# Query feature maps turned before the output projection in segment attention

## The reference

```
for each segment of 128 tokens (8 a sequence), 16 heads of 64:
    sq  = elu(q) + 1                                  # query feature map
    mem = mem + sq^T v;   zc = zc + sum(elu(k) + 1)
    att_dot = softmax(q k^T / 8) v
    att = gate * (sq mem / (sum(sq) * zc)) + (1 - gate) * att_dot
    out = att @ Wo                                    # output projection
x = layernorm(x + out)
```

## Time and profile before

| | us |
|---|---|
| median of 3 runs | 1880.17 |
| lowest, highest | 1877.43, 1881.06 |
| profiled execution | 1873.57 |
| its span | 1871.8 |
| segment attention in it, to the end of the last projection | about 798 |

### The profile page before, as it was taken

One profiled execution on the slowest core, in us unless ns is written; L12 is line 12 of the kernel. 1 busy time (PEld: TensorE's weight loads), 2 busy tenths in 40 slices (PEclk: granted clock), 3 DMA queues, 4 the chain that ended last, 5 costly groups with the idle time before them and its releaser, 6 DMA issues. The chain is left out here.

```text
span 1871.8 us, 43129 instructions
## 1 busy us (share of the span) xinstructions
PE 1764.5 (94%) x16161; PEld 1205.1 (64%) x16262; DVE 1441.4 (77%) x2680; ACT 1528.0 (82%) x4481; POOL 706.6 (38%) x814
## 2 busy tenths in 40 slices
PE   6999999999999999899999998899999999999995
PEld 5888888888888888759999997722222222222244
DVE  6677777777777777556666665599999999999957
ACT  6777777777777777648898865599999999999977
POOL 2344433334433444404766640032332333333325
PEclk9999999999999999999999999999999999999998
DMA  7332332232222232541101005833344335334202
GB/s 175 52 63 63 59 68 62 58 64 59 61 61 64 61 61 56 107 108 48 43 18 43 18 4 139 250 42 51 46 72 65 46 55 75 54 46 68 25 1 91
DMA packets 139775, 121.65 MB, mean 65 GB/s; under 512 B 78875, under 2 KB 111535, under 8 KB 139567
## 3 DMA queue, kind: packets, MB, share of 16 engines
q1 hardware_dynamic: 139567, 118.88, 32.2%
HBM read 77.29 MB, written 41.53 MB: 63 GB/s over the span
## 5 line engine op out<-in xcount | busy, mean ns | idle before, releaser
L2011 DVE TENSOR_REDUCE s_neg_max<-s_ring 128x1 f32<-128x1024 f32 x512 | 579.9, 1210 | 6.3 <-PE s_ring L1904 6.2
L1946 ACT ACTIVATE s_prob<-s_ring,s_neg_max 128x1024 f32<-128x1024 f32 x512 | 570.3, 1115 | 3.3 <-DVE s_neg_max L2011 2.2
L1917 PE MATMUL s_acc<-s_prob,s_v_norm 128*32 128x256 f32 x4096 | 326.6, 392 | 2.0 <-POOL s_v_norm L1988 2.0
L1904 PE MATMUL s_ring<-f_stack 128*128 128x512 bf16 x923 | 287.8, 385 | 27.2 <-issue 17.7
L1984 POOL TENSOR_TENSOR s_row_inv<-s_row_sum,s_neg_one 128x4 f32<-128x4 f32 x128 | 129.0, 1008 | 380.8 <-ACT s_prob L1946 380.8
L595 POOL TENSOR_SCALAR a_relu_ring<-a_qT 128x512 f32<-128x512 f32 x64 | 98.7, 1559 | 341.8 <-ACT a_qT L463 314.6
L1917 PEld LDWEIGHTS s_acc<-s_prob,s_v_norm 128*32 128x32 f32 x4096 | 81.5, 108 | 217.8 <-issue 214.3
L1904 PEld LDWEIGHTS s_ring<-f_stack 128*128 128x128 bf16 x1024 | 58.5, 97 | 232.5 <-ACT s_prob L1946 223.3
L492 ACT ACTIVATE a_prob<-a_psum,a_neg_max 128x128 f32<-128x128 f32 x512 | 179.9, 402 | 21.4 <-DVE a_neg_max L703 21.4
L746 DVE SCALAR_TENSOR_TENSOR a_att<-a_psum,a_keep_cols,a_num_s 128x128 f32<-128x128 f32 x256 | 72.2, 344 | 131.6 <-ACT a_num_s L518 131.5
L1289 ACT ACTIVATE x_prob<-x_psum,x_neg_max 128x77 f32<-128x77 f32 x512 | 160.8, 337 | 14.2 <-DVE x_neg_max L1445 14.1
(11 more groups left out here) (206 smaller groups left out, 4116.8 us busy)
## 6 DMA issues: line engine op xcount, KB each, us to landing
f_stack<-qk_thirds SPq DMA_DIRECT2D x256, 128.0 KB, 7.1
segment_values<-a_v_stage SPq DMA_DIRECT2D x64, 256.0 KB, 3.2
a_v_pos<-segment_values SPq DMA_DIRECT2D x512, 32.0 KB
qk_thirds<-p_third SPq DMA_DIRECT2D x16, 768.0 KB, 7.7
a_x_in<-in_x_dram SPq DMA_DIRECT2D x16, 256.0 KB, 3.3
a_x_res<-in_x_dram SPq DMA_DIRECT2D x32, 128.0 KB, 2.8
after_attention<-a_normed SPq DMA_DIRECT2D x32, 128.0 KB, 2.4
x_x_in<-after_attention SPq DMA_DIRECT2D x32, 128.0 KB, 2.0
```

The lines of the kernel that those rows point to most:

```text
L1904: last = pe.matmul(ring[n % 3][:, f * HALF:(f + 1) * HALF], k_stack[:, slot, j, kt * P:(kt + 1) * P], q_stack[:, slot, j, f * HALF:(f + 1) ...
L1917: last = pe.matmul(acc[32 * j:32 * j + 32, s], v_norm[:, step // KT % 2, step % 4, j, :], prob[:, step % 4, j, s], start=step % (2 * KT) = ...
L1946: act.activation(prob[:, step % 4, j, :], ring[n % 3][:, :], ACT.Exp, bias=neg_max[:, step % 2, j:j + 1], accum_out=row_sum[:, step % 4, j ...
L2011: dve.tensor_reduce(neg_max[:, step % 2, j:j + 1], ring[n % 3][:, :], AX_X, ALU.max, negate=True).then_inc(max_ready, 1)
```

## The change

In PE's preparation the first two turns of the query feature maps, `turn_phi(it, 0)` and `turn_phi(it, 1)`, stand directly behind scores 0 and 1, ahead of the first half of the output projection. Before, they stood behind it. No other engine's program is touched, and no wait or semaphore is changed. In pass 0, which has no projection there, the order is the same as before.

```
@@ -411,10 +411,10 @@
             def preparation(it):
                 scores(it, 0)
                 scores(it, 1)
+                turn_phi(it, 0)
+                turn_phi(it, 1)
                 if it > 0:
                     project_out(pe, it - 1, range(0, 8))
-                turn_phi(it, 0)
-                turn_phi(it, 1)
                 scores(it, 2)
                 if it > 0:
                     project_out(pe, it - 1, range(8, 12))
```

## The result

| | before, us | changed, us |
|---|---|---|
| median | 1877.77 (6 runs, 1874.99 to 1881.06) | 1915.36 (6 runs, 1908.94 to 1917.68) |
| profiled execution | 1873.57 | 1917.68 |
| its span | 1871.8 | 1915.9 |

The changed kernel is slower: ratio 1.0195, 95% interval 1.0178 to 1.0211. By the medians that is 37.6 us, where 21 were forecast; 1915.4 lies above the range (1895 to 1910). The sign was right, the size was not. The forecast stood on the 1880.2 of the three runs shown ahead of it; over six the median before is 2.4 us lower, so the miss in the difference, 37.6 against 21, is larger than that in the time.

What follows compares the result with a forecast made beforehand. PE was taken to bound the kernel: 14 passes at 1.37 us plus pass 2 at 1.93 make 21.1 us, which on a median of 1880.2 gives 1901.3 us, 1.1% slower. The range was 1895 to 1910.

Steps and rivals of the forecast that it cites:

- The sign: Whole kernel: the change makes it slower, by more than 0.2% (3.8 us), given 95%.
- What bounds the kernel: Segment-attention stage: PE has no room; each us more it idles costs one, unless another PE wait in the pass shrinks.
- Step 1, the wait: Before the first turn, passes 1 to 15: PE idles 1.92 us until the query feature map is ready.
- Step 2: Turns 0 and 1, then the projection: turns lose 0.21 us, projection's 0.20 wait goes; scores 2 start 1.93 us later.
- Step 3, what comes back: Turns 2 and 3 lose their 0.20 gap, memory's 0.56 wait shrinks; turns of normalised maps come 1.37 us later.
- Step 4: Rest of the pass after the normalised maps' turns: gives nothing back, adds zero, with bounds zero and 0.3 us.
- The clock: PE's clock: new 1.9 us idle times should not bring the 1.2 GHz level; zero in the sum.
- rival E: Turns and projection run at half speed in each pass: 15 x 4.67 = 70 us more, 1971 us; chance 1%.
- A: At memory unit 2, nothing comes back, the 0.56 wait returns: 1.93 or 1.73 a pass, 1906 to 1909 us; 20%.
- B: Later slack in the pass takes all old idle, 0.76 a pass: 17.6 us in all, 1898 us; chance 5%.
- C: ACT and DVE pace the pass, so PE's idle is free and 11.4 us goes: 1869 us; chance 2%.
- D: Before the first turn, maps are ready as scores end; no new wait, only 0.20 goes: 1877 us; chance 2%.

Runs made afterwards that it cites:

- the split at 4: Against the kernel before, the two turns stand after a quarter of the output projection (head positions 0 to 3): 1870.15 us, ratio 0.9957.
- the wait alone: Order of the kernel before; only the projection's first half also waits for the first query feature map, passes 1 to 15: 1917.26 us, ratio 1.0200.
- the kernel with `make_phi` first: Changed order on PE; on DVE `make_phi` 0 and 1 moved ahead of the row maxima of scores 0: 1887.50 us, ratio 1.0037 to before.

## Why the prediction was wrong

- *What bounds the kernel*: right. PE sets the pass; what it idled more was paid in every kernel above.
- *Step 1, the wait*: right to 0.01 us (1.93 against 1.92). Pass 0 as a gauge, 0.74 us from `make_phi` to the turn, held (440.62 to 441.36).
- *Step 2*: a little too dear. I forecast scores 2 1.93 us later; in pass 4 they come 244.54 - 235.81 = 8.73 after the scores' start instead of 6.92, 1.81 later. The projection followed by scores takes 3.56 where followed by transposes it took 3.65. And scores 2 followed by the projection take 0.89 instead of 1.00, as the transposes no longer stand ahead of them. I had moved these distances as they were, though they depend on the neighbour.
- *Step 3, what comes back*: right in its outcome. The gap at turns 2 and 3 is gone and memory waits 0.15. With step 2's error a pass at full clock costs 1.11 and not 1.37. Of the reasons, one was half of the story: the forecast had the scores later and DVE in time for them, and indeed DVE now waits for scores 2 (2.42 us above). But DVE also gets through sooner, as `make_phi` 2 is no longer slowed, and the split at 4 gets the same 0.15 with scores 3 at 10.78 us instead of 10.96. Pass 2 before, used as the measure of a ready DVE, already had that short `make_phi`.
- *Step 4*: right. The attention half has no new wait; 31.46 us from the turns of the normalised maps to the next pass in pass 4, 31.49 before.
- *The clock*: this is the step that failed. The sum had nothing for it ("New idle times of 1.9 us among full work should not bring that") and rival E had 1%. It is 19.8 of 37 us, shown by three kinds of kernel: fill the wait and it is gone, keep the wait without the new order and it is there, shorten the wait and it is gone. The slip was to take one pass of one execution as a proof. Seven other kernels here have the same program in pass 0, and in the trace of each of them the granted clock of pass 0 falls below 1.00 (0.93 to 0.96 from 33 to 80 us, where before it is 1.00); in six of them it does so already in the stretch of the earlier trace rows, 33 to 50 us. With the split at 4 the scores of unit 3 in pass 0 are such a row (1.16 us in the clear passes):

```profile
43.27 2.08 PE L298 MATMUL a_psum<-a_kT,a_qT 64*128 64x128 f32 x16
```

  So the calm of pass 0 was luck, one execution in eight. Which of the fifteen passes stay clear is not settled by these runs: in the changed kernel 4, 9 and 14, at even distances, with the wait alone 1, 3, 10 and 15.
- *The size of rival E*: 4.67 us a pass supposed that turns and projection run at half speed from end to end. The stretch is shorter: it cost 1.65.
- *The page of the skill*: the Trainium skill, "TensorE: Matmul & The Clock Gate", section "A second HAM failure mode: psum-queue depth-cycling", has short idle times between groups of matmuls make the clock swing and cost throughput. I set it below the row of pass 0. The trace agrees in that a short idle time was followed by the lower clock, 12 times in 15, and cost time; but it was one idle time of 1.93 us in a pass of 50, not a frequent one.
- *Rivals A to D*: none came. In the changed kernel memory never waited 0.56 (A), the attention half gave nothing back and 0.15 stayed at memory (B; that its 1.17 a pass lies near the 1.11 of a clear pass is luck, by the distances of step 2), PE's idle time was paid in every clear pass (C), and the maps were not ready as the scores ended (D).

With the measured clock term put in, the forecast's own sum is 21.1 + 12 x 1.65 = 40.9 us, and 37.0 with the measured 1.11 and 1.68 as well. The price and the number of the stretches are readings of the changed kernel; no row of before gave them.

## What to carry to other kernels

A step moved ahead on the engine that bounds the kernel must find its inputs ready: take from the timeline when they are made, and put just so much other work ahead of it that covers this (here a quarter of a projection, 1.83 us, turned some 37 us lost into some 8 won, by the ratio 0.9957). Idle time of some 2 us on TensorE, in work like this, is to be priced at its length plus a chance of a half-speed stretch behind it, and one calm pass in one execution is no proof against it. Useless matmuls in a gap that can't be closed are a quick test for the clock, and can be a cure.

## What was not expected of the hardware

With 1.93 us of idle time in a pass 12 of 15 passes had a stretch at the 1.2 GHz level behind it; with 1.25, 0.81, 0.59 or 0.48 us none had one behind the turns. That is no bound for idle time in general: in the attention half of pass 15, where PE waits five times 0.77 us, these four kernels and the split at 4 have a stretch each, the others none. It costs more: to the last projection that pass takes 42.27 us with 12 transposes in the gap, 39.55 with the wait alone.

A stretch behind the new wait cost 1.54 to 1.69 us in the changed kernel, and about the same, 1.7 (1.9 once), with the wait alone; so it made little difference whether transposes or the projection came first.

The `make_phi` of unit 2 took 1.55 us in most passes before and 0.68 after the change (444.34 above; longest of all 64 in the changed kernel 0.93 us, before 1.56). Passes 7 and 2 of the kernel before, the same instructions in the same order, DVE and POOL (its multiplication of the probabilities, L611, two of them merged):

```profile
375.94 1.55 DVE L668 SCALAR_TENSOR_TENSOR a_e_ring<-a_e_ring,a_relu_ring 128x512 f32<-128x512 f32 x1
375.91 2.48 POOL L611 TENSOR_TENSOR a_prob<-a_prob,a_row_inv 128x512 f32<-128x512 f32 x2
...
136.11 0.69 DVE L668 SCALAR_TENSOR_TENSOR a_e_ring<-a_e_ring,a_relu_ring 128x512 f32<-128x512 f32 x1
136.13 3.01 POOL L611 TENSOR_TENSOR a_prob<-a_prob,a_row_inv 128x512 f32<-128x512 f32 x2
```

In pass 7 `make_phi` begins 0.03 us behind POOL and is the one that lasts long; in pass 2 it begins 0.02 ahead, and POOL's pair lasts 0.53 longer. After the change it begins 0.33 us ahead. Where POOL had begun 0.03, 0.31, 0.39 or 0.76 us before (passes 7 and 8 before, the kernel with `make_phi` first, pass 1 with the wait alone), `make_phi` took 1.55, 1.28, 1.20 and 0.83 us: each time it ended 0.55 us after POOL's first multiplication of 1.04 us. So by these rows the one that starts second waits for the other's end, and a shift of 0.05 us decides over 0.86 us of DVE and 0.4 at PE's memory products. POOL's other operation, the positive part (L595), did not lengthen it: in the changed kernel one runs from 1.13 us before the 0.68 us `make_phi` of pass 8 to 0.35 behind its start. The Trainium skill, "Perfetto Trace Analysis", section "Optimizing Scalar/DVE Operations", says that GpSimd and VectorE share an SBUF read port; these durations agree, but no run here took POOL's work away to show it.
